# Trigonometric attention in a two-layer decoder: angles for eight heads at once, rows moved by DMA, masks by products on TensorE

## What is computed

```python
pos = theta / TWO_PI % 1.0 * TABLE_SIZE
i0f = jnp.floor(pos)
frac = pos - i0f
s = SIN_T[i0] * (1.0 - frac) + SIN_T[i1] * frac      # and c from COS_T
...
theta_q = xh / (1.0 + jnp.abs(w_q)) + b_q + t * phi_q
Q = jnp.concatenate([cos_q, sin_q], axis=-1)         # K alike
V = cos_v + sin_v                                    # no t * phi
scores = jnp.einsum('bqhd,bkhd->bhqk', Q, K) / scale
scores = jnp.where(causal, -jnp.inf, scores)
attn = jax.nn.softmax(scores, axis=-1)
out = jnp.einsum('bhqk,bkhd->bqhd', attn, V).reshape(B, S, D)
theta_out = out / (1.0 + jnp.abs(w_out)) + b_out     # then cos + sin again
```

## Time and profile before

| | us |
|---|---|
| median of 3 runs | 1048.44 |
| lowest, highest | 1045.14, 1050.01 |
| the profiled execution | 1045.22 |
| its span, first to last instruction | 1043.5 |
| end of the first attention in it | 278.65 |

### The profile page before, as it was taken

How to read it: one execution, slowest core, us unless ns; L and a number is a source line. 1 busy time by engine, 2 the same in 40 slices (tenths; PEclk the granted TensorE clock), 3 DMA queues, 4 the chain that set the end, 5 groups by cost and what they waited for, 6 DMA issues and landing times. The chain is left out here.

```text
span 1043.5 us, 20376 instructions
## 1 busy us (share of the span) xinstructions
PE 913.1 (88%) x8028; PEld 565.3 (54%) x8028; DVE 754.9 (72%) x1412; ACT 601.3 (58%) x1052; POOL 350.1 (34%) x310
## 2 busy tenths in 40 slices
PE   2778878899589799999689999998799988999996
PEld 1323333333247545565456777776699974455554
DVE  8957978895778899887768899886678865344412
ACT  4778969999567553552145555554688853332410
POOL 1314764563237231000246667675243210000000
PEclk9969989999779999999999999999899999999999
DMA  5000000000221030000130000000200000000001
GB/s 145 0 2 1 1 2 1 1 1 1 67 96 42 1 133 1 1 2 1 46 120 2 2 1 2 3 2 1 72 2 1 3 1 1 1 13 9 21 1 41
DMA packets 17502, 21.96 MB, mean 21 GB/s; under 512 B 4656, under 2 KB 14590, under 8 KB 17024
## 3 DMA queue, kind: packets, MB, share of 16 engines
q1 hardware_dynamic: 15296, 18.57, 5.5%
q10 hardware_dynamic: 2112, 2.10, 0.6%
HBM read 18.56 MB, written 2.10 MB: 20 GB/s over the span
## 5 line engine op out<-in xcount | busy, mean ns | idle before, releaser
L625 PE MATMUL t_sc<-t_qk 32*128 32x512 f32 (+3 forms) x768 | 117.2, 571 | 41.4 <-ACT t_pT L515 16.2
L515 ACT ACTIVATE t_pT<-t_sc 128x1536 f32<-128x1536 f32 x96 | 136.7, 1453 | 23.8 <-PE t_sc L625 22.9
L3081 DVE SCALAR_TENSOR_TENSOR f_h<-f_psh,f_h 128x512 f16<-128x512 f32 x64 | 43.9, 691 | 100.8 <-ACT f_h L3107 100.7
L3137 PE MATMUL f_psh<-f_h,fs_w 128*128 128x512 f16 x512 | 114.4, 379 | 1.5 <-DVE f_h L3081 1.5
L229 POOL TENSOR_SCALAR_AFFINE_SELECT t_pT<-t_pT 128x512 f32<-128x512 f32 x64 | 75.1, 1196 | 112.7 <-ACT t_pT L515 112.4
L625 PEld LDWEIGHTS t_sc<-t_qk 32*128 32x128 f32 x768 | 53.2, 203 | 104.9 <-ACT t_pT L515 61.3
L3107 ACT ACTIVATE f_h<-f_psh 128x512 f16<-128x512 f32 x64 | 38.2, 597 | 108.4 <-PE f_psh L3137 108.4
L2600 POOL TENSOR_SCALAR_AFFINE_SELECT r_att<-r_att 128x1024 f16<-128x1024 f16 x64 | 69.6, 1110 | 66.2 <-DVE r_att L2640 66.0
L645 PE MATMUL t_ot<-t_pT,t_v 128*17 128x512 f32 (+3 forms) x768 | 73.6, 511 | 9.4 <-issue 8.8
L3137 PEld LDWEIGHTS f_psh<-f_h,fs_w 128*128 128x128 f16 x512 | 49.8, 98 | 59.0 <-issue 2.0
L1896 PE MATMUL c_pso<-ck_VO,c_pT 128*128 128x256 f16 x480 | 55.0, 273 | 1.4 <-DVE c_pT L1747 1.4
(11 more groups left out here) (504 smaller groups left out, 2175.2 us busy)
## 6 DMA issues: line engine op xcount, KB each, us to landing
x<-in_x ACTq DMA_DIRECT2D x4, 512.0 KB, 7.6
out_x<-x SPq DMA_DIRECT2D x4, 512.0 KB, 2.9
r_rcos<-in_ret_cos SPq DMA_DIRECT2D x1, 1280.0 KB, 8.0
r_rsin<-in_ret_sin SPq DMA_DIRECT2D x1, 1280.0 KB, 10.5
gw_raw<-in_gateT SPq DMA_DIRECT2D x1, 1024.0 KB, 7.1
gw_raw<-in_upT SPq DMA_DIRECT2D x1, 1024.0 KB, 9.1
gw_raw<-in_downT SPq DMA_DIRECT2D x1, 1024.0 KB, 4.7
fs_k<-in_L_ffn_k SPq DMA_DIRECT2D x1, 1024.0 KB, 7.4
```

Source lines behind the costliest of these rows:

```text
L515: a.activation(pT[:, at:at + 3, :].rearrange("p a s -> p (a s)"), sc[n % 2][:], ACT.Exp, scale=CURVE * CURVE / math.sqrt(2 * DH)).then_inc ...
L625: last = t.matmul(sc[n % 2][:, 512 * k + at:512 * k + at + w], qk[r, g % 2, 1, P * i:P * i + P], qk[r, g % 2, 0, q0:q0 + w], start=(part = ...
L3081: v.scalar_tensor_tensor(dst[:, 1], psh[:, i % BANKS, :], 0.0, dst[:, 0], ALU.max, ALU.subtract).then_inc(lo_done, 1)
L3137: last = mm(psh[:, i % BANKS, :], l, r, start=(k == 0), stop=(k == len(todo) - 1))
```

## The change

Turn steps go over groups of eight heads (128 columns of xn, not doubled) instead of quads. The angle is made once; its sine gives the sine rows, and the sine of a quarter turn minus its absolute value (`distance`) the cosine rows, both on all 128 partitions. Since the cosine and sine rows of a head now lie 16 by 16 in two tiles, SP copies them to their places in `qk`, 16 partitions in each DMA (`move`); `qk` has three buffers. The distance is squared on DVE, in f16. V and the output angles are made in parts of eight heads. POOL has no masks and squares left; instead PE adds the product of an identity and a bf16 matrix of -1e14 above the diagonal to each diagonal block of the scores, before the exponential. The sines stand in one block on ACT after the second exponential of each odd quad, and the weighs are spread over the fills by `between`. The batch 1 rows are normalised on DVE.

```diff
-        xn = sb("xn", [P, NT, H0, 2, DH])
+        ident_low, future = sb("ident_low", [P, P], BF16), sb("future", [P, P], BF16)
+        xn = sb("xn", [P, NT, D])
         trow = sb("trow", [P, S])
-        angle = sb("angle", [P, 2, 2 * S])
-        frac = sb("frac", [P, 2, 2 * S])
-        tmp = sb("tmp", [P, 2 * S])
-        qk = sb("qk", [P, 2, 2, S])
+        sines = sb("sines", [P, 2 * S])
+        cosines = sb("cosines", [P, 2 * S])
+        frac = sb("frac", [P, 2 * S], F16)
+        tmp = sb("tmp", [P, S])
+        qk = sb("qk", [P, 3, 2, S])
-        TURN_AT = [8] + [2] * (QUADS - 1)
-        STEPS = [("turn", 0, 0), ("turn", 0, 1), ("turn", 1, None)]
+        GROUPS = QUADS // 2
+        TURN_AT = {(0, 8): 1, (2, 2): 2, (4, 2): 3}
+        STEPS = [("turn", 0, 0), ("turn", 0, 1)]
         for g in range(QUADS):
             for e in range(EXPS):
-                if e == TURN_AT[g] and g + 2 < QUADS:
-                    STEPS.append(("turn", g + 2, None))
+                if (g, e) in TURN_AT:
+                    STEPS.append(("turn", TURN_AT[g, e], None))
...
+            def move(g, c, lo, hi, done):
+
+                for hh in range(4):
+                    at = 64 * (g % 2) + 16 * hh
+                    src = (cosines, sines)[c][at:at + 16, :].rearrange("p (k s) -> p k s", k=2)
+                    sp.dma_start(qk[32 * hh + 16 * c:32 * hh + 16 * c + 16, g % 3, :, lo:hi], src[:, :, lo:hi]).then_inc(done, 16)
+
+            for h in range(2):
+                for g in range(2):
+                    for c in range(2):
+                        if g == 0:
+                            sp.wait_ge(bent, 2 * pieces_of(0, h) - 1 + c)
+                        move(g, c, 512 * h, 512 * h + 512, moved[g] if h or g else first)
+            for n in range(1, GROUPS):
+                for g in (2 * n, 2 * n + 1):
+                    if g >= 3:
+                        sp.wait_ge(filled, LAST_EXP(g - 3))
+                    for c in range(2):
+                        if g == 2 * n:
+                            sp.wait_ge(bent, 2 * pieces_of(n) - 1 + c)
+                        move(g, c, 0, S, moved[g % 3])
...
-            def mask(slot):
-                at = 4 * slot % RING
-                g.wait_ge(stepped, AT[("exp", exps_for(slot), None)] + 1)
-                for c in DIAGONAL[slot % SLOTS]:
-                    blk = pT[:, at:at + 4, c:c + P]
-                    last = g.affine_select(out=blk, in_=blk, compare_op=ALU.is_ge, fill=0.0, base=0,
-                                           pattern=[[0, 4], [1, P]], channel_multiplier=-1)
-                last.then_inc(masked, 1)
+            own.link(g.memset(ident_low[:], 0.0))
+            g.affine_select(out=ident_low[:], in_=ident_low[:], compare_op=ALU.not_equal, fill=1.0, base=0,
+                            pattern=[[-1, P]], channel_multiplier=1).then_inc(future_ready, 1)
+            own.link(g.memset(future[:], 0.0))
+            g.affine_select(out=future[:], in_=future[:], compare_op=ALU.is_ge, fill=FUTURE, base=0,
+                            pattern=[[1, P]], channel_multiplier=-1).then_inc(future_ready, 1)
...
                 L(v.tensor_scalar(t_, a, ROUND_TURN, ROUND_TURN, ALU.add, ALU.subtract))
-                L(v.scalar_tensor_tensor(a, a, -0.5, t_, ALU.add, ALU.subtract))
+                L(v.tensor_tensor(a, a, t_, ALU.subtract))
 
             def fraction(a, f, t_):
-                L(v.tensor_scalar(t_, a, ROUND1, None, ALU.add))
-                return v.scalar_tensor_tensor(f, t_, ROUND1, a, ALU.subtract, ALU.subtract)
+                L(v.tensor_scalar(t_, a, -0.5, ROUND1, ALU.add, ALU.add))
+                L(v.scalar_tensor_tensor(f, t_, ROUND1, a, ALU.subtract, ALU.subtract))
+                L(v.tensor_scalar(f, f, 0.5, None, ALU.add))
+
+            def square(f):
+                return v.tensor_tensor(f, f, f, ALU.mult)
...
+            def distance(n, h=None):
+
+                v.tensor_scalar(piece(cosines, h).bitcast(U32), piece(sines, h).bitcast(U32), 0x7FFFFFFF, None, ALU.bitwise_and).then_inc(cos_pre, 1)
+
+            def post_qk(n, h=None):
+                f = piece(frac, h)
+                v.wait_ge(sin_pre, pieces_of(n, h))
+                for w, waves in ((cosines, cos_waves), (sines, sin_waves)):
+                    v.wait_ge(waves, pieces_of(n, h))
+                    v.scalar_tensor_tensor(piece(w, h), f, CURVE_OFF, piece(w, h), ALU.add, ALU.mult).then_inc(bent, 1)
...
+                L(v.tensor_tensor(a4, rows_, by_head(rrow[:, 0, :]), ALU.mult))
+                L(v.tensor_tensor(a4, a4, by_head(rows[:, 1, :]), ALU.add))
+                whole_turns(va[:], tmp[:])
+                fraction(va[:], vf[:], tmp[:])
+                square(vf[:]).then_inc(v_pre, 1)
...
+            for h in range(2):
+                a, f = piece(sines, h), piece(frac, h)
+                t_ = tmp[:].rearrange("p (k s) -> p k s", k=2)
+                angles(0, h)
+                whole_turns(a, t_)
+                distance(0, h)
+                fraction(a, f, t_)
+                square(f).then_inc(sin_pre, 1)
+                if h == 0:
+                    post_qk(0, 0)
...
+            row_gains(0, 0, 1, slice(0, 128))
             post_qk(0, 1)
+            variances(1)
             pre_v(0)
+            row_gains(0, 0, 1, slice(128, D))
+            row_gains(1, 2, 3, slice(0, D))
+            v.wait_ge(rs_ready, 2)
+            v.wait_ge(mean_ready, 2)
+            normalise(TB, 2 * TB, xn_next)
             post_v(0)
+            pre_v(1)
+
+            def prepare(n):
+                v.wait_ge(bent, 2 * pieces_of(n - 1))
+                angles(n)
+                whole_turns(sines[:], cosines[:])
+
+            def prepare_rest(n):
+                fraction(sines[:], frac[:], cosines[:])
+                distance(n)
+                square(frac[:]).then_inc(sin_pre, 1)
+
+            prepare(1)
+            prepare_rest(1)
+                n = g // 2 + 1
+                if g % 2 == 0:
+                    if n < GROUPS:
+                        prepare(n)
+                    front_o(g - 1, 0)
+                    if n < GROUPS:
+                        prepare_rest(n)
+                    front_o(g - 1, 1)
+                    pre_o(n - 2)
+                else:
+                    front_o(g - 1, 0)
+                    if n < GROUPS:
+                        post_qk(n)
+                        post_v(n)
+                        if n + 1 < GROUPS:
+                            pre_v(n + 1)
+                    front_o(g - 1, 1)
+                    if g == QUADS - 1:
+                        pre_o(3)
+                    if n >= 2:
+                        post_o(n - 2)
...
+                if n:
+                    for g in (2 * n - 2, 2 * n - 1):
+                        a.wait_ge(moved[g % 3], moves_of(g))
+                if n == 1:
+                    a.wait_ge(first, 16 * 8)
...
+            def waves_qk(n, h=None):
+                cut = lambda w: w[:] if h is None else w[:].rearrange("p (k s) -> p k s", k=2)[:, :, 512 * h:512 * h + 512]
+                a.wait_ge(cos_pre, pieces_of(n, h))
+                a.activation(cut(cosines), cut(cosines), ACT.Sin, bias=quarter[:], scale=-SIN_SCALE).then_inc(cos_waves, 1)
+                waves(sin_pre, pieces_of(n, h), sin_waves, cut(sines))
...
+                    if (g, e) in TURN_AT:
+                        turn_step(TURN_AT[g, e])
                     exp_step(EXPS * g + e)
+                    if (g, e) == (0, 7):
+                        waves_v(0)
+                    if g % 2 and e == 1:
+                        n = g // 2 + 1
+                        if n < GROUPS:
+                            waves_qk(n)
+                            waves_v(n)
+                        if n >= 2:
+                            waves_o(n - 2)
+                    if g and e == (3 if g % 2 else 5):
                         copy_o(g - 1, 1)
+                    if e == (10 if g % 2 or not g else 11):
...
+                    t.wait_ge(future_ready, 2)
+                    t.wait_ge(first, 16 * 8)
+                if e == 2 or g and e % EXPS == 0:
+                    t.wait_ge(moved[g % 3], moves_of(g))
...
+                for slot, h, k in chunks:
+                    for j, i, at, w in PIECES[slot % SLOTS]:
+                        if P * i == 512 * j + 512 - w:
+                            last = t.matmul(sc[s % 2][:, 512 * k + at:512 * k + at + P], ident_low[:], future[:],
+                                            start=False, stop=True, skip_group_check=True)
...
+            def between(g, e):
+                here, past = SLOTS * g, SLOTS * (g - 1)
+                if g == 0:
+                    return {8: range(0, 6), 11: range(6, 7)}.get(e, ())
+                if g % 2 == 0:
+                    return {0: (past + 4,), 1: (past + 5,), 2: (past + 6, past + 7), 3: (past + 8,),
```

(59 more changed lines are left out.)

361 lines of the change are left out of this document (112 added, 249 removed).

## The result

The changed kernel takes 1055.34 us (median of 5 runs, 1053.43 to 1060.01) beside 1047.71 us (1045.14 to 1050.01) for the kernel before: a ratio of 1.0081, interval 1.006 to 1.0102, so slower by 6.3 to 10.7 us. The profiled execution took 1053.43 us with a span of 1051.7, 8.2 more than before. The first attention now ends at 285.87 + 0.42 = 286.29 us instead of 278.65: 7.6 of the 8.2.

The account below looks back on a forecast made before the run. PE and ACT were taken to bound the first attention, both within some 10% of full. Quads from 2 on +6.1 and the start -0.2 gave +5.9; with 1045.2 + 1.6 that made 1052.7 us, range 1038 to 1066.

Parts of the forecast that it names:

- the sum: Whole kernel: net slowdown of 5.9 us, from +6.1 for quads 2 to 7 and -0.2 for what precedes them.
- Masks on PE: 32 mask products in each quad, 0.055 us each plus 0.11 a group, add 2.5 us a quad on PE.
- Rival (a): First attention's fills: masks fit into gaps the fills leave, saving 12 us, so -6 net, 1040.8 us; chance 0.20.
- (b): Each of 56 mask groups on PE waits out its neighbours' tails, 0.17 us more each: +15, 1062.2 us; chance 0.20.
- Even quads: First attention: 27.2 us of PE work, plus waits of 0.6 for an exponential and 1.1 for front_o: 28.9 us.
- Odd quads: First attention, bound by ACT: 3.5 us, then an 8.7 us sine block, then 17.2 us of exponentials and copies: 29.4 us.
- last list: Signs to check in the changed kernel's trace, including late row moves, half clock after 80 us and DVE waits over 1 us.
- Quads 6 and 7: End of the first attention: 26.7 us without turn or preparation, then 37.0 with a short block, last weighs and tail.
- +6.1: From quad 2's first exponential to the first attention's end: 180.3 us instead of 174.2.
- The start: Before quad 2: row moves make exponential 2 some 12 us late, at 46.0, but the lag is given back by 104.2.
- The term of -0.2: Up to quad 2's first exponential: 104.2 us instead of 104.40, the early lag being given back.
- Rival (c): Before quad 2: PE's clock rises sooner and row moves may issue faster, -5, so +1 net, 1047.7 us; chance 0.12.

## Why the prediction was right, and where it wasn't

The time (1055.34 in 1038 to 1066), the sign and the forecast's mechanism held; the sum was short, 5.9 against the 8.2 us between the two profiled executions and the 6.3 to 10.7 of the ratio.

- *Masks on PE.* 0.055 a product and 0.11 a group were taken; 0.055 and about 0.1 were measured (0.01 for the group ahead of transposes), and the 0.055 again when doubled. Rival (a), masks in the fills' gaps, and (b), drains in full, fall by the same rows. The 12 us that (a) would have saved are about what leaving the masks out gave (10 to 13).
- *Even quads.* Forecast 28.9, measured 28.2. The work was right (27.2 against 27.1 busy); of the 1.7 us of waits 1.1 were there. DVE reached the second front_o almost in time: 0.4 us a quad and not 1.1.
- *Odd quads.* Forecast 29.4, measured 31.0 and 30.6. The wait of 4 us behind the block was right (4.64, 3.77, 3.77). The step that failed is what stands behind it: ten exponentials in 17.2 us, priced with fills of 1.06, took 19.4 in quad 3. The prediction's own last list named a clock at half after 80 us as a thing that would make it wrong; it was there, and its 1.6 and 1.2 us were partly made up by the even quads. The earlier trace rows had shown the half clock at the start, and it was read as a matter of the start alone, when it should have been asked of each wait that the change makes, and of the 3.23 us wait that it does away with.
- *Quads 6 and 7.* 26.7 and 37.0 forecast, 26.6 and 37.2 measured. In all the quads: 181.9 instead of 180.3, so +7.6 where the sum has +6.1.
- *The start.* Rows out and landed, exponential 2, end of exponential 7, exponential 8, quad 2: forecast 30, 46.0, 57.5, 63.6, 104.2; measured 30.4, 45.9, 57.5, 63.9, 104.4. Two errors cancelled: SP took 0.63 to 0.67 us to issue a move, not 0.5, and 64 KB landed after 2.3 us, not 3. The f16 operations of 2048 columns took 0.69 and 1.22, taken as 0.65 and 1.15.
- *The start, as a cause.* The term of -0.2 was right, and yet the start held 3.4 us, since the order of DVE's and SP's work inside it was taken as given. Rival (c), a clock that rises sooner there, was real as a mechanism but needed zero products to bring the clock up, and alone kept one or two of its microseconds.
- *The other signs.* Two more of the last list came and cost nothing. The moves of 128 KB landed 5.6 to 6.9 us after issue (medians), over the 5 that were named, yet PE waited for none of them after quad 0. And DVE waited up to 15.2 us in quads 2 to 5, for ACT, while PE waited at most 0.4 for `front_o`. As signs of being wrong they were badly chosen.
- *The rest of the program*, taken at nothing, was 0.6, which can't be told from nothing.

## What to carry to other kernels

When a change makes TensorE wait longer in one place, price what follows the wait at its lower clock as well, and look for such stretches in the kernel before, since the change may remove one: here a wait of 4 us cost some 2.5 us more in each pair of quads, and a row of useless products in it bought that back. What is left of the wait has to be short: 1.09 us left over did no harm, while 3.60 us at one place and 2.25 at another undid the filling. An operation moved to an engine that is 86% busy is paid by a good part of what it takes there, however small each piece is: here 10 to 13 of 20 us, in pieces of 0.055. And a single profile can hold microseconds of the clock that the next execution doesn't: read a small difference from the ratio of many.

## What the runs showed of the hardware beyond that

- The granted clock in the windows of these traces can't be trusted before its first change: it reads 1.00 from 30 to 58 us in the changed kernel, where fills take 2.08 us. With sixteen zero products ahead, the same fills at the same length stand beside 0.50. The length of a known product is the safer witness. The Trainium skill (TensorE: Matmul & The Clock Gate, Part 1) warns that clock events in traces have been seen unreliable; this may be such a case, though no run here tells why the rows read so.
- The clock can stay at half while PE is busy without a gap: in the kernel before six fills in a row took 11.06 us, 0.46 us of waiting ahead of them, while in the changed kernel with the whole wait filled the same fills took 1.13 each from the first.
- A DMA share of 1.0 from row moves inside SBUF slowed neither PE nor ACT: in the kernel with the wait filled, fills of 1.13 and exponentials of 1.45 us stood beside a share of 1.09.
- The same program loses more or less to the clock from one execution to the next: quad 5 took 30.6 us in one trace, at a mean clock of 0.89 from 194 to 224 us, and 32.0 in two others, at 0.83, though they run the same code there.
